# Output projection accumulated pair by pair in two PSUM banks, with three projections sharing two banks and a new order of the feed-forward stages

## The reference, cut to what matters

```python
# x: (4, 2048, 256), 16 heads of 64; layer norm without weights = _layernorm
xn = _layer_norm(x, gamma, beta)
Q, K, V = xn @ WQ.T + bQ, xn @ WK.T + bK, xn @ WV.T + bV
gate = silu(xn @ Wg.T + bg);  alpha = sigmoid(alpha_logit)
h = alpha * h + k v^T;  o = q h                    # step by step over the 2048 tokens, per head
y = x + (o * gate) @ WO.T + bO
x1 = _layernorm(x + y)
gf = global_net(mean of x1 over the tokens)        # 256 -> 128 -> 64 -> 1
out = x1
for _ in range(3):                                 # coupling_net: 256 -> 256 -> 128 -> 64 -> 1
    combined = 0.7 * gf + 0.3 * coupling_net(out)
    out = out + (0.1 + adaptive_range * (combined - 0.5) * 2.0) * twist(out)
result = _layernorm(x1 + out)
```

## Time and profile before

| | us |
|---|---|
| median of 3 runs | 1919.58 (1919.38 to 1921.05) |
| profiled execution, its own time | 1920.54 |
| its span | 1918.8 |
| TensorE busy | 1836.1 (96%) |
| VectorE busy | 1081.2 (56%) |
| ScalarE busy | 711.3 (37%) |
| output projection, L875, 1024 instructions | 226.3 |
| gate product, L721, 128 instructions | 88.5 (0.69 each) |
| next input's low part, L585, one of a supertile | 1.22 |
| mean granted TensorE clock | 0.986 |

### The profile page before, as it was taken

The page is one execution under the profiler, slowest core; times in us unless marked ns, Lnnn a source line. Parts: engine busy times, 40 slices in busy tenths (PEclk is TensorE's granted clock), DMA queues, the critical chain, the costliest instruction groups (busy, mean ns, idle before and its releaser), DMA issues.

```text
span 1918.8 us, 44137 instructions
## 1 busy us (share of the span) xinstructions
PE 1836.1 (96%) x19178; PEld 1408.3 (73%) x19178; DVE 1081.2 (56%) x2230; ACT 711.3 (37%) x1297; POOL 315.5 (16%) x246
## 2 busy tenths in 40 slices
PE   5999999999799999999989999999979999999996
PEld 4888888853588888884378888888338888888732
DVE  7646465644764655554665556565376565555546
ACT  3424242434442424234443233333444333324344
POOL 3111111102211111210221212021022021211002
PEclk9999999999899999999989999999999999999998
DMA  4000000000100000000010000000001000000001
GB/s 158 2 12 2 13 2 12 3 0 1 56 2 12 2 12 2 12 2 1 0 56 2 12 2 13 1 13 1 1 11 46 2 13 2 13 2 13 1 0 45
DMA packets 23345, 26.65 MB, mean 14 GB/s; under 512 B 3184, under 2 KB 22000, under 8 KB 23152
## 3 DMA queue, kind: packets, MB, share of 16 engines
q1 hardware_dynamic: 21152, 19.62, 3.2%
q10 hardware_dynamic: 2000, 4.20, 0.6%
HBM read 15.42 MB, written 8.39 MB: 12 GB/s over the span
## 4 chain that ended last, share of the span: by engine, by line
PE 87%; DVE 10%; ACT 2%; issue 1%; DMA 0%; POOL 0%; DVEq 0%; ACTq 0%; SPq 0%
PE bank L803 38%; PE bank L875 12%; PE bank L1029 8%; PE bank L866 7%; PE bank L830 6%; PE bank L857 6%; DVE x_nf L764 4%; PE bank L847 3%; DVE v_sb L771 3%; PE bank L839 3%; PE bank L1072 1%; DVE cpl L760 1%; PE bank L794 1%; DVE stats L557 1%; PE bank L1046 1%; PE bank L885 1%
## 5 line engine op out<-in xcount | busy, mean ns | idle before, releaser
L415 ACT ACTIVATE q_sb<-q_sb,pows 128x384 f32<-128x384 f32 (+2 forms) x387 | 168.7, 498 | 450.4 <-DVE q_sb L599 450.4
L721 DVE TENSOR_TENSOR o_g<-bank,gate 128x512 f32<-128x512 f32 x128 | 88.5, 691 | 438.4 <-PE bank L866 438.4
L345 POOL TENSOR_TENSOR k_end<-k_sc,pows 128x512 f32<-128x512 f32 x129 | 136.0, 1054 | 779.9 <-DVE k_sc L590 779.9
L433 ACT ACTIVATE h_bd<-h_seq,pows 64x256 f32<-64x256 f32 x256 | 129.9, 507 | 349.8 <-DVE h_seq L699 346.6
L875 PE MATMUL bank<-wo,o_g 128*128 128x256 f32 x1024 | 226.3, 379 | 0.0
L875 PEld LDWEIGHTS bank<-wo,o_g 128*128 128x128 f32 x1024 | 193.3, 190 | 26.1
L683 DVE COPY_PREDICATED att<-causal,bank 128x1024 f32<-128x1024 int32 x128 | 168.2, 1314 | 8.5 <-PE bank L830 8.0
L857 PEld LDWEIGHTS bank<-q_sb,h_bd 128*128 128x128 f32 x1024 | 134.1, 191 | 10.6
L866 PE MATMUL bank<-att,v_sb 128*64 128x128 f32 x2048 | 140.1, 279 | 0.0
L857 PE MATMUL bank<-q_sb,h_bd 128*128 128x128 f32 x1024 | 134.8, 275 | 0.0
L1029 PE MATMUL bank<-v_sb,f_w 128*128 128x512 f32 x256 | 118.4, 605 | 12.7 <-DVE v_sb L771 12.7
(11 more groups left out here) (136 smaller groups left out, 3351.8 us busy)
## 6 DMA issues: line engine op xcount, KB each, us to landing
x_in<-in_x SPq DMA_DIRECT2D x17, 512.0 KB, 4.0
out_y<-o_g SPq DMA_DIRECT2D x16, 512.0 KB, 2.9
v_sb<-in_wq ACTq DMA_DIRECT2D x1, 1024.0 KB, 5.0
v_sb<-in_wk SPq DMA_DIRECT2D x1, 1024.0 KB, 5.7
o_g<-in_wg ACTq DMA_DIRECT2D x1, 1024.0 KB, 9.3
o_g<-in_wv ACTq DMA_DIRECT2D x1, 1024.0 KB, 12.1
wo<-in_wo ACTq DMA_DIRECT2D x1, 1024.0 KB, 16.0
bias_v<-in_bV SPq DMA_DIRECT2D x1, 512.0 KB, 8.1
```

The source lines that it names most:

```text
L345: nc.gpsimd.tensor_tensor(k_end[:].rearrange("p (a z) (b r) -> p a (z b) r", z=2, r=BL), k_sc[:].rearrange("p (a z) (b r) -> p a (z b) r", ...
L415: last = nc.scalar.activation(q_sb[:, p % 2, d].rearrange("p (a z) n -> p a (z n)", z=2)[:, :, reach], q_sb[:, p % 2, 0].rearrange("p (a z ...
L433: nc.scalar.activation(h_bd[rows, :, e * DH:(e + 1) * DH], h_seq[rows, :, :], ACT.Copy, scale=pows[rows, p, HP:HP + 1]).then_inc(s_hbd, 1)
```

## The change: what it does

- `o_g` keeps two pairs instead of eight. `y_part(p, n)` adds one pair for all four chunks, into banks 6 and 7, and is issued in each pair's iteration: after the g projection of pair p + 1 TensorE adds pair p - 1. Pair 7 is added at the supertile's end. The gate product waits until the pair before the last has been added (`s_yp`).
- k and q share banks 0 and 1 and change places from pair to pair, and g goes into the bank that k of the same pair has just left: g of p + 1 waits for `keys_of(p + 1)` (`s_kev`), which it did not before. Updates share bank 4 with the transposed keys.
- The supertile's end: `x_transposed` stands in pair 6, after `keys_transposed`; `project("k", 0)` stands in pair 7 between `from_state` and `from_chunk`; q and g come after `from_chunk`; the last `y_part` is the last thing. VectorE does the next input's low part before `masked(7)`. The additions of y into `x_2b` come after that, and the first two value evacuations of the next supertile follow the statistics.
- `values` uses banks 2, 3, 5, 1, 2, 3, 0, 5, so some values wait for earlier ones' evacuation; the third waits for the third stored tile of the batch before (`s_fin`, b * NS - 1), and only the first `y_part` of the batch waits for the fourth.
- `x1_transposed` is issued once for each supertile, in pair 0 of the next one, into banks 6 and 7, or at the feed-forward start for the batch's last.
- In the last supertile of all, the load, statistics, transposes and projections of a further input are left out (`following`).
- Feed-forward order: after layer 2 of visit n comes a half of the first tile's layer 1 of visit n + 1, after layer 3 its other half, and the second tile's layer 1 comes after layer 4. `h1` holds one visit's tiles in the second half of `q_sb`; `fin` uses the same place and `x_nf`.

Lines removed from the functions printed above are left out below.

```diff
...
-        o_g = sb("o_g", [P, NP, ST])
+        o_g = sb("o_g", [P, 2, ST])
...
-        h1 = o_g[:].rearrange("p (t m) n -> p t m n", m=2)
+        spare = q_sb[:, 1].rearrange("p b c n -> p (b c n)")
+        h1 = spare.rearrange("p (t m n) -> p t m n", t=GT, m=2)
...
-        fin = o_g[:].rearrange("p (t m) (c d) -> p t (m c) d", t=NS, d=D)
+        fin = [tile.rearrange("p (t c d) -> p t c d", t=2, d=D)[:, i]
+               for tile in (spare, x_nf[:].rearrange("p a n -> p (a n)")) for i in range(2)]
...
+        def k_bank(p):
+
+            return p % 2
+
+        def q_bank(p):
+
+            return 1 - p % 2
+
+        def g_bank(n):
+
+            return n % NP % 2 if n else 5
...
-        order = [(1, 0, range(GT))]
+        order = [(1, 0, [(j, m) for j in range(GT) for m in range(2)])]
         for n in range(VIS):
             more = n + 1 < VIS
-            order += [(2, n, range(GT))] + [(1, n + 1, [0])] * more + [(3, n, range(GT))] + [(1, n + 1, [1])] * more
-            order += [(4, n, range(GT))]
+            order += [(2, n, range(GT))] + [(1, n + 1, [(0, 0)])] * more
+            order += [(3, n, range(GT))] + [(1, n + 1, [(0, 1)])] * more
+            order += [(4, n, range(GT))] + [(1, n + 1, [(1, 0), (1, 1)])] * more
...
-            return bank[(2, 3, 1, 4, 5, 6, 7, 0)[m]]
+            return bank[(2, 3, 5, 1, 2, 3, 0, 5)[m]]
...
+                        n = it * NP + p
+                        if p + 1 < NP:
+                            ends_of(p + 1, n + 1)
+                        elif following:
+                            ends_of(0, n + 1)
...
-                    x1_copied(b, s, (s + NS - 1) % NS)
+                    following = it + 1 < B * NS
+                    tokens_of(it * NP, 4)
                     for p in range(NP):
                         n = it * NP + p
                         states_of(p, n)
@@ -478,27 +500,30 @@
                             act.wait_ge(s_og, n + C0)
                             gate_of(p + 1, n + 1)
                             tokens_of(n + 1, 4)
+                            if p == 0 and s:
+                                x1_copied(it - 1, 6)
+                            if p == NP - 2 and following:
+                                x_parts(it + 1, (0, 1))
                         else:
-                            act.wait_ge(s_g, n + 1)
-                            x_parts(it + 1, (0, 1))
-                            queries_shifted(0, n + 1)
-                            act.wait_ge(s_og, n + C0)
-                            gate_of(0, n + 1)
+                            if following:
+                                queries_shifted(0, n + 1)
+                            if following:
...
+            def gated(p, n):
+
+                dve.wait_ge(s_o, n + 1 + C0)
+                dve.wait_ge(s_gev, n + 1)
+                dve.wait_ge(s_yp, n - 1 + C0)
+                nc.vector.tensor_tensor(o_g[:, p % 2], bank[5], gate[:, p % 2, :], ALU.mult).then_inc(s_og, 1)
...
+                        if p + 1 < NP:
+                            if p:
+                                masked(n)
+                            keys_of(p + 1, n + 1)
+                            if p == 0:
+                                dve.wait_ge(s_out, b * NS * 16 + C0)
+                            queries_of(p + 1, n + 1)
+                            if p == NP - 5 and following:
+                                input_stats(it + 1, b * STC + (2 * s + 1) * ST1)
+                            if p == NP - 3 and following:
+                                input_norm(it + 1, it * KT + C0)
+                            gated(p, n)
+                        else:
+                            if following:
+                                low_part(it + 1)
                             masked(n)
-                        if p + 1 < NP:
-                            keys_of(p + 1, n + 1)
-                            queries_of(p + 1, n + 1)
+                            if following:
+                                keys_of(0, n + 1)
+                            gated(p, n)
+                            if following:
+                                queries_of(0, n + 1)
+
+                    for h in range(2):
+                        if h == 0:
+                            dve.wait_ge(s_y, it + 1)
                         else:
-                            low_part(it + 1)
-                        if p == NP - 5:
-                            input_stats(it + 1, b * STC + (2 * s + 1) * ST1)
-                        if p == NP - 3:
-                            input_norm(it + 1, (b * (NS + 1) + s + 1) * KT + C0)
-                        dve.wait_ge(s_o, n + 1 + C0)
-                        dve.wait_ge(s_gev, n + 1)
-                        if p == 0:
-                            dve.wait_ge(s_out, b * NS * 16 + C0)
-                        nc.vector.tensor_tensor(o_g[:, p, :], bank[5], gate[:, p % 2, :],
-                                                ALU.mult).then_inc(s_og, 1)
-
-                    queries_of(0, (it + 1) * NP)
-                    for h in range(2):
-                        dve.wait_ge(s_y, it * 2 + h + 1)
+                            dve.wait_ge(s_yp, (it + 1) * NP + C0)
                         dve.wait_ge(s_x2b, it * 2 + 2)
                         nc.vector.tensor_tensor(x_2b[:, 2 * h:2 * h + 2, :], x_2b[:, 2 * h:2 * h + 2, :],
-                                                part(7 * (1 - h), 2), ALU.add).then_inc(s_r, 1)
+                                                part(6 + h, 2), ALU.add).then_inc(s_r, 1)
...
+                    norm_stats(lambda c: x_2b[:, c, :], b * STC + (2 * s + 1 + following) * ST1, s_r1)
+                    if s + 1 < NS:
+                        for m in range(2):
+                            values_kept(it + 1, m)
...
+            def y_part(p, n):
+
+                pe.wait_ge(s_og, n + 1 + C0)
+                for c in range(NC):
+                    tok = slice(c * C, (c + 1) * C)
+                    dst = bank[6 + c // 2][:, (c % 2) * D:(c % 2 + 1) * D]
+                    last = nc.tensor.matmul(dst, o_g[:, p % 2, tok], wo[:, p, :], start=(p == 0 and c % 2 == 0),
+                                            stop=(p == NP - 1), skip_group_check=True)
+                    if p == NP - 1 and c == 1:
+                        last.then_inc(s_y, 1)
+                last.then_inc(s_yp, 1)
...
             for b in range(B):
                 for s in range(NS):
                     it = b * NS + s
+                    following = it + 1 < B * NS
                     pe.wait_ge(s_att, it * NP + C0)
                     pe.wait_ge(s_fin, b * NS - 3 + CF)
                     for m in range(2 * NC):
                         if m == 2:
+                            pe.wait_ge(s_og, it * NP + C0)
+                            pe.wait_ge(s_fin, b * NS - 1 + CF)
+                            if it == 0:
+                                pe.wait_ge(s_gev, 1)
+                        if m == 3:
                             pe.wait_ge(s_qev, it * NP + 1 + C0)
                         if m == 4:
+                            pe.wait_ge(s_vev, it * 2 * NC + 1)
+                        if m == 5:
+                            pe.wait_ge(s_vev, it * 2 * NC + 2)
+                        if m == 6:
+                            pe.wait_ge(s_gev, it * NP + 1)
+                            pe.wait_ge(s_kev, it * NP + 1 + C0)
+                        if m == 7:
+                            pe.wait_ge(s_vev, it * 2 * NC + 3)
+                        values(m).then_inc(s_v, 1)
                         if m == 5:
                             pe.wait_ge(s_hend, it * NP + C0)
                             pe.wait_ge(s_kend, it * NP + 1 + C0)
+                            keys_transposed(4).then_inc(s_kt, 1)
                     pe.wait_ge(s_setv, 15)
                     pe.wait_ge(s_const, 16 * len(consts))
                     for p in range(NP):
                         n = it * NP + p
                         if p == 0:
                             pe.wait_ge(s_qsh, n + 1 + C0)
+                            pe.wait_ge(s_vev, it * 2 * NC + 6)
+                            scores(p).then_inc(s_score, 1)
                             pe.wait_ge(s_ktok, n + 1 + C0)
                             pe.wait_ge(s_vev, it * 2 * NC + 2 * NC)
                             updates(p).then_inc(s_upd, 1)
                         if p + 1 < NP:
                             pe.wait_ge(s_qev, n + 1 + C0)
+                            project("k", p + 1, k_bank(p + 1)).then_inc(s_k, 1)
                             pe.wait_ge(s_gev, n + 1)
+                            project("q", p + 1, q_bank(p + 1)).then_inc(s_q, 1)
+                            pe.wait_ge(s_kev, n + 2 + C0)
+                            project("g", p + 1, g_bank(p + 1)).then_inc(s_g, 1)
+                        if p == 1:
+                            pe.wait_ge(s_wo, 16)
```

(39 more changed lines are left out.)

176 lines of the change are left out of this document (55 added, 121 removed).

## The result

The changed kernel takes 1892.28 us (median of 4 runs, 1891.71 to 1892.58) against 1919.58: a ratio of 0.9856, 95% interval 0.9839 to 0.9873. The forecast was 1907.9, with a range of 1899 to 1917. The sign was right, the size was not: 27.3 us came instead of 11.7.

The account below looks back on a forecast made before the run. TensorE's queue was taken to bound the supertiles, with short waits on VectorE in the feed-forward part and VectorE's chain at batch ends. Gains 24.0 less costs 12.3 made 11.7 us: 1919.58 to 1907.9, range 1899 to 1917.

Parts of the forecast that it names:

- Feed-forward waits: Feed-forward part: TensorE's 24 waits before layer 1 on VectorE's updates all go, a gain of 12.7 us.
- Batch's end: Feed-forward end: VectorE's chain starts 3.43 earlier but runs 2.2 to 2.3 later within; gain 1.1 a batch, 4.5 us.
- rival (c): Feed-forward part: halved cover brings new waits before layers 3 and 4, 0.5 a visit; 1919.9 us, chance 0.08.
- The costs of the moves: Supertiles: y blocks 1.1, keys 2.9 and 5.2, `from_state(7)` 1.6, values after y 1.5; 12.3 us in all.
- y blocks and the values' load: Supertiles: 0.01 more per y block, 1.1 us, and an exposed load for the values after y, 1.5 us.
- Keys in 96 pairs: Pairs 1 to 6: g's weight load waits for the keys, 0.03 a pair, 2.9 us; upper end 9.6.
- Pair 0: Pair 0 of 13 supertiles: keys end 0.24 after g's start; with hand-over and exposed load 0.40 each, 5.2 us.
- `from_state(7)`: Supertile's end: the state operand is about 0.1 late, bounds 0 and 0.4; 16 x 0.1 = 1.6 us.
- Rival (b): Supertiles: weight loads hidden and y blocks free, only 3.1 and 1.5 paid; 1900.2 us, chance 0.20.
- Rival (d): Moves cost more than taken (y blocks 7.8, keys 6, the end 5); 1915 to 1916 us, chance 0.14.
- The weight load across a wait: g's load after the keys' semaphore: if pulled ahead of the wait, the costs' sum would be 4.2 us lower.
- Rival (a): Every pair: the keys decide, 0.40 in all 96 pairs, 38.4 us instead of 2.9; 1943 us, chance 0.08.

Follow-up runs that it names:

- ffn_order_only: The kernel before with the new order of the feed-forward layers and nothing else: 1898.41 us, ratio 0.9886.
- keys_late_512: The changed kernel with a VectorE fill of 128x512 (0.49 us) ahead of the keys' scaling in pairs 1 to 6: 1928.94 us, ratio 1.0049.

## Why the prediction was wrong

**Feed-forward waits: right in mechanism, the term mis-sized.** "All 24 waits go: 12.7 us" took the list's sum. All 24 went, and they were worth 17.6. The prediction had said that matmuls must be priced by the distance between starts, and left that rule for the one term where a list was at hand. Against the same distances without a wait each of the 24 cost 0.62 to 0.85 us; the list has 0.5 to 0.6.

**Batch's end.** Visit 5's coupling was forecast 12.7 after layer 4 and came at 12.75; the chain was to start 3.43 earlier and did. The rest of the difference to 4.5 is rounding of 10.6 and 12.7: 3.43 - 2.18 = 1.25 a batch. Nothing became late before layers 3 and 4, so rival (c) is out.

**The costs of the moves: the failed step.** 12.3 us was forecast, 0.85 measured. In its parts:
- y blocks and the values' load: "I take 0.01" a block, 1.1 in all, and 1.5 for the load. From each y block to the next instruction's start are 220.4 us in all against 222.4, 2.0 less; the value projections take 138.5 against 136.4, 2.1 more. A block behind g costs 1.72 or 1.73, the one in pair 7, behind the scores, 1.83, and the last of a supertile 1.54, the rest of it going to the values' first load. So the 1.5 was the same time counted a second time; both ends together cost 0.2 instead of 2.6.
- Keys in 96 pairs: the working was right. It found the load at 149.76 and 0.1 to go, "just in time for 149.89", and then put 0.03 a pair on it for safety, 2.9 us. A wait that just fits costs nothing: by the row the keys ended 0.19 before g's turn, which the rule prices at zero. In the change's list of weight-load waits the keys stand with 23:

```profile
PEld bank L848 <- DVE k_sc L615: 8.4, 23, 0.4
```

Sixteen of them are pair 0. Of the 7 in pairs 1 to 6, four (0.38 to 0.40 us listed) cost about 0.2 each, and three (0.15 to 0.16 listed) nothing. The 96 pairs together take as long from k to the end of g as before, within 0.1 us.
- Pair 0: the price was right (0.15 on top of the lateness; 0.17 measured), the lateness was not. 0.24 was read from before, and it was 0.07 after. From the first scores to g's turn are 4.44 us in both kernels, but the masked scores start 1.14 after them and not 1.28, and everything on VectorE follows. Why they do is open; nothing was tried on it. So 0.24 instead of 0.40, 13 x 0.24 = 3.1 instead of 5.2.
- `from_state(7)`: 1.6 forecast, no wait of a matmul in the trace. That row was bounded by 0 and 0.4, and 0.1 taken.

So four doubtful costs, each with a bound at or near zero, were each taken above it, 7.1 us in all, and came to about nothing. Pair 0 was 2.1 too dear. The last 2.4 us are a term that the prediction had at nothing: blocks that stand beside other neighbours than before. From start to start, in the supertiles in the middle of a batch, `from_state(7)` takes 0.17 less (0.81 for 0.98), the three blocks of transposed keys, which have other work behind them now, 0.27 less together, g of pair 0 0.10 less, k of pair 0 0.18 more, and the transposes of x1 and of the input 0.17 and 0.04 more. That is -0.15 in each of 16 supertiles. It is a sum of the trace and near its noise: in ffn_order_only, whose supertiles are those of before, each is about 0.07 shorter.

Together these make the 11.4 of the 16.3 us missed, and the wait term makes 4.9; the rest nearly cancels. Rival (b), "the costs stay out", described this part with 1900.2. Its 3.1 for pair 0 came, its 1.5 for the values' load did not; with the waits at 17.6 it would have said 1895.3. Rival (d) was added up wrong: its three terms (7.8, 6 and 5, for 1.1, 2.9 and 3.1) give 1919.6 and not 1915 to 1916; nothing of it came.

**The weight load across a wait.** The prediction weighed a rule of the Trainium skill (TensorE: Matmul & The Clock Gate, the row on the engine queue in its first table: loads are pulled ahead of matmuls in flight). If it held across a semaphore wait, g's load would not have seen the keys. It sees them: in keys_late_512 it starts at 151.24, 0.06 after they end, with its other operand long there. The costs stayed out for another reason, the load's 0.11 of room.

**Right:** the last supertile (4.4 and 4.33, with the wait of 0.8 on the gate product), the layer norm of x1 in time, no new wait of a matmul in the feed-forward part. Rival (a), 1943, needed 0.15 a pair. keys_late_512 shows that its mechanism exists 0.43 us further on (the keys' end from -0.19 to +0.24), and that it would indeed have turned the change into a loss: 1928.94.

## What to carry to other kernels

Price a wait of TensorE that goes away by the distance between starts with and without it; the listed idle time was 0.07 to 0.27 short of it in the three cases read here. Where a new wait just fits by your own working, write zero and keep the upper end for the range; a few hundredths "for safety" in each of a hundred pairs are a forecast of their own. And before you price a wait in a moved block, ask for the end of what it waits for against the first weight load's turn, not the matmul's: here the load had to start 0.11 us ahead.
